# Graph attention layer with a feed-forward step: the low halves of four weights on another engine, four banks for the skip tiles, and three smaller edits

## The reference, cut to what matters

```python
xn = layernorm(x)                                   # x: 1250 x 512
q, k, v = [(xn @ W + b).reshape(n, 4, 512) for W, b in ((Wq, bq), (Wk, bk), (Wv, bv))]
alpha = einsum('ehc,ehc->eh', q[dst], k[src]) / sqrt(512)       # 20000 edges
attn = softmax of alpha over the edges with the same dst
agg = segment_sum(attn[:, :, None] * v[src], dst).reshape(n, 2048)
x_attn = agg + xn @ Wskip + bskip
h = x_attn @ Wlin + blin + x_attn[:, :512]
x = x + gamma * (h - mean(h)) / sqrt(var(h) + 1e-5) + beta
z = layernorm(x)
x = x + z, with one-hot results of three small MLPs on decoded bits of z added in columns 80 to 111
```

## Time and profile before

| | |
|---|---|
| median of 3 runs | 1007.43 us (1007.0 to 1008.04) |
| the profiled execution's own time | 1006.13 us |
| its span, first to last instruction | 1004.1 us |
| granted TensorE clock, mean | 0.995 of full speed |
| busy: TensorE, DVE, ACT, POOL | 985.0, 579.6, 337.0, 105.3 us |
| TensorE's share of the chain that ended last | 94% |

### The profile page before, as it was taken

The page is one execution under the profiler, slowest core; times in us unless marked ns, Lnnn a source line. Parts: engine busy times, 40 slices in busy tenths (PEclk is TensorE's granted clock), DMA queues, the critical chain, the costliest instruction groups (busy, mean ns, idle before and its releaser), DMA issues.

```text
span 1004.1 us, 13119 instructions
## 1 busy us (share of the span) xinstructions
PE 985.0 (98%) x4841; PEld 804.6 (80%) x4841; DVE 579.6 (58%) x1224; ACT 337.0 (34%) x530; POOL 105.3 (10%) x232
## 2 busy tenths in 40 slices
PE   9999999999999999999999999999999999999994
PEld 6677767588888888888888888888888888888883
DVE  6999987452455455226454542354455325788786
ACT  4447555102223223114222321133232213445353
POOL 2121101000000000000000000000000000344465
PEclk9999999999999999999999999999999999999997
DMA  9856654400152335004323430161334103443421
GB/s 328 301 193 210 246 187 165 169 1 1 52 189 62 97 98 169 28 1 147 121 79 105 154 88 1 27 214 54 105 79 163 52 1 82 154 125 100 143 82 40
DMA packets 43048, 115.82 MB, mean 115 GB/s; under 512 B 4960, under 2 KB 25306, under 8 KB 39660
## 3 DMA queue, kind: packets, MB, share of 16 engines
q1 hardware_dynamic: 38380, 98.20, 31.3%
q0 software_dynamic: 4608, 16.78, 4.3%
HBM read 70.07 MB, written 44.90 MB: 114 GB/s over the span
## 4 chain that ended last, share of the span: by engine, by line
PE 94%; DVE 3%; DMA 1%; issue 1%; ACT 0%; SPq 0%; DVEq 0%
PE ps_o L1513 10%; PE ps_o L1514 10%; PE ps_o L1515 10%; PE ps_r L1513 9%; PE ps_r L1514 9%; PE ps_r L1515 9%; PE ps_s L1514 9%; PE ps_s L1515 9%; PE ps_s L1513 9%; PE ps_t L1513 2%; PE ps_t L1515 2%; PE ps_t L1514 2%; PE ps_s L1632 1%; PE ps_s L1592 1%; DMA early<-in_Wv 1%
## 5 line engine op out<-in xcount | busy, mean ns | idle before, releaser
L1514 PE MATMUL ps_s<-xT_lo,tT 128*128 128x512 f32 (+1 forms) x480 | 168.7, 351 | 0.0
L1515 PE MATMUL ps_s<-xT_hi,tT 128*128 128x512 f32 (+1 forms) x480 | 168.4, 351 | 0.0
L1513 PE MATMUL ps_s<-xT_hi,tT 128*128 128x512 f32 (+1 forms) x480 | 168.1, 350 | 0.0
L1513 PE MATMUL ps_o<-y,pT 128*128 128x512 f32 x380 | 148.6, 391 | 0.0
L1514 PE MATMUL ps_o<-y,pT 128*128 128x512 f32 x380 | 148.0, 389 | 0.0
L1515 PE MATMUL ps_o<-y,pT 128*128 128x512 f32 x380 | 148.0, 389 | 0.0
L881 ACT ACTIVATE prob<-prob,nbias 128x1250 f32<-128x1250 f32 x40 | 53.7, 1342 | 267.8 <-DVE nbias L1277 267.8
L1271 DVE CUSTOM_DVE_ANT_0 prob<-ps_s,maskb 128x1250 f32<-128x1250 f32 x40 | 58.2, 1455 | 128.0 <-issue 127.8
L1513 PEld LDWEIGHTS ps_s<-xT_hi,tT 128*128 128x128 f32 x480 | 90.6, 189 | 14.3 <-issue 0.3
L1514 PEld LDWEIGHTS ps_s<-xT_lo,tT 128*128 128x128 f32 x480 | 90.6, 189 | 13.9
L1515 PEld LDWEIGHTS ps_s<-xT_hi,tT 128*128 128x128 f32 x480 | 90.7, 189 | 12.6
(11 more groups left out here) (289 smaller groups left out, 1761.1 us busy)
## 6 DMA issues: line engine op xcount, KB each, us to landing
regrouped<-prob SPq DMA_DIRECT2D x156, 160.0 KB, 2.8
whole<-regrouped SPq DMA_DIRECT2D x39, 640.0 KB, 3.9
products<-prod_parts POOLq DMA_DIRECT2D x32, 512.0 KB, 3.8
gbuf<-products SPq DMA_DIRECT2D x4, 2048.0 KB, 8.2
mbuf<-products SPq DMA_DIRECT2D x4, 2048.0 KB, 9.1
stage<-in_Wskip SPq DMA_DIRECT2D x4, 1024.0 KB, 5.3
stage<-in_Wq SPq DMA_DIRECT2D x3, 1024.0 KB, 5.2
stage<-in_Wk SPq DMA_DIRECT2D x3, 1024.0 KB, 5.9
```

Source lines behind the costliest of these rows:

```text
L1513: nc.tensor.matmul(out_, a[0], b[0], start=start, stop=False)
L1514: nc.tensor.matmul(out_, a[0], b[1], start=False, stop=False)
L1515: return nc.tensor.matmul(out_, a[1], b[0], start=False, stop=stop)
```

## The change

- **Low halves.** For `n` = 4, 9, 14, 19, POOL forms the low half, by one operation of 128x2048 behind its store of block 0 of products 1, 4, 7 and 10. DVE no longer does.
- **Skip banks.** The skip tiles go through four banks (ps_r 0, ps_o, ps_t 0, ps_t 1). TensorE waits for DVE's adds from tile 4 on, and once for the last saved block of the products.
- **Counts of product 1.** Part 0 after block 1, part 1 after block 2, parts 2 and 3 after block 3.
- **Operand 3 in halves.** Its high and low halves are each formed by columns in two operations, as for operand 2.
- **Tail.** The sum of squares takes the raw row sum (scaled by 512) in place of the mean, so it comes before the mean in ACT's list; the centring on DVE and the second layernorm's factors wait for the mean.
- **Last stores.** Tiles 8 and 9 are stored in three pieces each: the two beside columns 80 to 111 when the row is scaled, and these 32 columns when the results are in, tile 9 first.

```diff
+SKIP_BANKS = 4
@@ skip_bank
-            return ps_r[0:R, 0, :] if t % 2 == 0 else ps_o[0:R, :]
+            return (ps_r[0:R, 0, :], ps_o[0:R, :], ps_t[0:R, 0, :], ps_t[0:R, 1, :])[t % SKIP_BANKS]
@@ sync
+            def store_rest(t):
+                rows = min(R, N - R * t)
+                sp.wait_ge(o_scaled, t + 1)
+                for a, b in ((LO_HI_OUT + 32, D), (0, LO_HI_OUT)):
+                    sp.dma_start(out[R * t:R * t + rows, a:b], acc[0:rows, t, a:b]).then_inc(out_done, 16)
+
+            def store_result(t):
+                rows = min(R, N - R * t)
+                some = slice(LO_HI_OUT, LO_HI_OUT + 32)
                 if t == BY_POOL:
                     sp.wait_ge(o_pool, 1)
                 else:
-                    sp.wait_ge(o_ready, t + 1 if t < BY_POOL else t)
+                    sp.wait_ge(o_ready, t)
+                sp.dma_start(out[R * t:R * t + rows, some], acc[0:rows, t, some]).then_inc(out_done, 16)
...
-            for t in range(NT - 4, NT):
+            for t in range(NT - 4, NT - 2):
                 store(t)
+            for t in range(NT - 2, NT):
+                store_rest(t)
+            for t in (NT - 1, NT - 2):
+                store_result(t)
@@ gpsimd
+            def skip_weight_lo(n):
+
+                pool.wait_ge(hi_ready[n % 2], n // 2)
+                nc.gpsimd.tensor_tensor(opnd[n % 4][1][:], raw(n)[:], opnd[n % 4][0][:].bitcast(F32),
+                                        ALU.subtract).then_inc(split_ready[n % 2], 1)
+
             for p in range(3 * H):
                 for i in range(KC):
                     if p % 3 != K_PROD:
                         store_product(p, i)
+                    if p % 3 == M_PROD and i == 0:
+                        skip_weight_lo(operands(p + 1)[0])
...
-                link(nc.gpsimd.tensor_scalar(veps[0:R, t:t + 1], stats[0:R, t, square:square + 1], 1.0 / D, EPS,
+                link(nc.gpsimd.tensor_scalar(veps[0:R, t:t + 1], stats[0:R, t, square:square + 1], 1.0 / D ** 3, EPS,
@@ scalar
+            def split_hi_halves(n):
+
+                for half, high in enumerate((half_hi[n - 2], hi_ready[n % 2])):
+                    some = half_cols(half)
+                    nc.scalar.activation(opnd[n][0][:, :, some], raw(n)[:, :, some], ACT.Copy).then_inc(high, 1)
+
+            act.wait_ge(diag_ready, 1)
+            split_hi_halves(3)
             act.wait_ge(early_in[0], 16)
-            nc.scalar.activation(opnd[2][0][:, :, half_cols(0)], raw(2)[:, :, half_cols(0)],
...
+            split_hi_halves(2)
@@ h_squares (z_squares in the same way, with res_ready)
                 act.wait_ge(acc_ready, NT * H + t + 1)
+                nc.scalar.activation(junk[0][0:R, :], acc[0:R, t, :], ACT.Square, scale=-float(D), bias=stats[0:R, t, 0:1],
+                                     accum_out=stats[0:R, t, 1:2]).then_inc(h_square, 1)
                 nc.scalar.activation(mv[0:R, t, 0:1], stats[0:R, t, 0:1], ACT.Copy, scale=1.0 / D).then_inc(h_mean, 1)
-                act.wait_ge(h_mean, t + 1)
-                nc.scalar.activation(junk[0:R, :], acc[0:R, t, :], ACT.Square, scale=-1.0, bias=mv[0:R, t, 0:1],
-                                     accum_out=stats[0:R, t, 1:2]).then_inc(h_square, 1)
@@ vector
-            split_lo(1, 1)
+            split_lo_halves(3)
...
-                elif i < 2 and p + 1 < 3 * H:
+                elif i < 2 and p + 1 < 3 * H and p % 3 != M_PROD:
                     split_lo(p + 1, 1 - i)
@@ tensor
                 if 0 < p <= NT and (p, i) != (1, 0):
-                    for some in ((0, 1) if (p, i) == (1, 1) else (i,)):
+                    for some in {(1, 1): (0,), (1, 2): (1,), (1, 3): (2, 3)}.get((p, i), (i,)):
                         count_part(p - 1, some)
...
             skip_part(1, (2, 3))
+            pe.wait_ge(prod_free, 12 * H)
             pe.wait_ge(total_ready, 1)
...
             for t in range(2, NT):
-                pe.wait_ge(skip_free, t - 1)
+                if t >= SKIP_BANKS:
+                    pe.wait_ge(skip_free, t - SKIP_BANKS + 1)
                 skip_part(t, range(KC))
```

More of the change, by code:

```diff
@@ L274, in graph_layer @@
         z_low = [put(f"z_low{i}", [P, Z_LOW], F32) for i in range(2)]
-        junk = put("junk", [P, D], BF16)
+        junk = [put(f"junk{i}", [P, D], BF16) for i in range(2)]
         flag_pool = put("flag_pool", [P, 4], F32)
@@ L347, in graph_layer @@
         split_ready = [sem(f"split_ready{i}") for i in range(2)]
-        half_hi, half_split = sem("half_hi"), sem("half_split")
+        half_hi, half_split = [sem(f"half_hi{n}") for n in (2, 3)], sem("half_split")
         prod_done, prod_hi, prod_free = sem("prod_done"), sem("prod_hi"), sem("prod_free")
@@ L552, in load_x @@
                              x[R * t:R * t + rows, :]).then_inc(xres_in[2 if t == NT - 1 else t % 2], 16)
-            def store(t):
+            def store_rest(t):
                 rows = min(R, N - R * t)
+                sp.wait_ge(o_scaled, t + 1)
[4 more added lines that the diff above has]
+                some = slice(LO_HI_OUT, LO_HI_OUT + 32)
                 if t == BY_POOL:
@@ L558, in store @@
                 else:
-                    sp.wait_ge(o_ready, t + 1 if t < BY_POOL else t)
+                    sp.wait_ge(o_ready, t)
+                sp.dma_start(out[R * t:R * t + rows, some], acc[0:rows, t, some]).then_inc(out_done, 16)
+            def store(t):
+                rows = min(R, N - R * t)
+                sp.wait_ge(o_ready, t + 1)
                 sp.dma_start(out[R * t:R * t + rows, :], acc[0:rows, t, :]).then_inc(out_done, 16)
@@ L576, in _ @@
                     load_x(NT - 1)
-            for t in range(NT - 4, NT):
+            for t in range(NT - 4, NT - 2):
                 store(t)
-            sp.wait_ge(out_done, 16 * NT)
+            for t in range(NT - 2, NT):
+                store_rest(t)
+            for t in (NT - 1, NT - 2):
+                store_result(t)
+            sp.wait_ge(out_done, 16 * (NT + 4))
         @block.gpsimd
@@ L658, in z_factors @@
                 nc.gpsimd.tensor_scalar(stats[0:R, t, 4:5], rstd[0:R, t:t + 1], 1.0, None, ALU.add)
+                pool.wait_ge(z_mean, t + 1)
                 nc.gpsimd.tensor_scalar(nmr[0:R, t:t + 1], mv[0:R, t, 1:2], rstd[0:R, t:t + 1], -1.0,
@@ L750, in split_hi @@
                     if n % 2 == odd:
[L751 to L758, removed]
+                        act.wait_ge(stage_in[odd], 16 * (n // 2 - 1))
+                        act.wait_ge(prod_done, 4 * last_use(n - 4) + 4)
                         nc.scalar.activation(opnd[n % 4][0][:], raw(n)[:], ACT.Copy).then_inc(hi_ready[odd], 1)
@@ L891, in h_squares @@
                 act.wait_ge(acc_ready, NT * H + t + 1)
+                nc.scalar.activation(junk[0][0:R, :], acc[0:R, t, :], ACT.Square, scale=-float(D), bias=stats[0:R, t, 0:1],
+                                     accum_out=stats[0:R, t, 1:2]).then_inc(h_square, 1)
                 nc.scalar.activation(mv[0:R, t, 0:1], stats[0:R, t, 0:1], ACT.Copy, scale=1.0 / D).then_inc(h_mean, 1)
-                act.wait_ge(h_mean, t + 1)
-                nc.scalar.activation(junk[0:R, :], acc[0:R, t, :], ACT.Square, scale=-1.0, bias=mv[0:R, t, 0:1],
-                                     accum_out=stats[0:R, t, 1:2]).then_inc(h_square, 1)
             def z_squares(t):
                 act.wait_ge(res_ready, t + 1)
+                nc.scalar.activation(junk[1][0:R, :], acc[0:R, t, :], ACT.Square, scale=-float(D), bias=stats[0:R, t, 2:3],
+                                     accum_out=stats[0:R, t, 3:4]).then_inc(z_square, 1)
                 nc.scalar.activation(mv[0:R, t, 1:2], stats[0:R, t, 2:3], ACT.Copy, scale=1.0 / D).then_inc(z_mean, 1)
-                act.wait_ge(z_mean, t + 1)
-                nc.scalar.activation(junk[0:R, :], acc[0:R, t, :], ACT.Square, scale=-1.0, bias=mv[0:R, t, 1:2],
-                                     accum_out=stats[0:R, t, 3:4]).then_inc(z_square, 1)
             def scale_rows(t):
@@ L999, in split_lo, with split_lo_halves @@
                                                 ALU.subtract).then_inc(split_ready[odd], 1)
-            def split_halves():
-                for some, high, low in ((half_cols(0), half_hi, half_split), (half_cols(1), hi_ready[0], split_ready[0])):
+            def split_lo_halves(n):
+                for half, high in enumerate((half_hi[n - 2], hi_ready[n % 2])):
+                    some = half_cols(half)
                     dve.wait_ge(high, 1)
-                    nc.vector.tensor_tensor(opnd[2][1][:, :, some], raw(2)[:, :, some],
-                                            opnd[2][0][:, :, some].bitcast(F32), ALU.subtract).then_inc(low, 1)
+                    ins = nc.vector.tensor_tensor(opnd[n][1][:, :, some], raw(n)[:, :, some],
+                                                  opnd[n][0][:, :, some].bitcast(F32), ALU.subtract)
+                    if half:
+                        ins.then_inc(split_ready[n % 2], 1)
```

(7 more changed lines are left out.)

4 lines of the change are left out of this document (removed).

## The result

The changed kernel takes 1012.99 us (median of 6 runs, 1012.5 to 1013.16), the kernel before 1008.18 beside it (6 runs, 1007.0 to 1008.7): ratio 1.0049, 95% interval 1.0036 to 1.0061. It is slower by more than the 0.2% that the prediction set, and outside its range (1004.2 to 1010.6). The profiled execution took 1012.94 us for a span of 1010.8; the one of before had a span of 1004.1, so the two traces are 6.7 us apart.

What follows compares the result with a forecast made beforehand. TensorE was taken as the bound, busy 985.0 of 1004.1 us, with gains only where it waits. Terms 0.95 + 1.25 + 0.2 - 2.5 + 0.5 - 0.85 = -0.45 us gave 1007.0 from 1007.43; range 1004.2 to 1010.6.

Steps and rivals of the forecast that it cites:

- Whom POOL's pass stops: POOL and DVE: whoever comes first keeps the other out if DVE reads two SBUF operands, as `onehot_src` does.
- the 0.95 predicted: Low half on POOL in product 1: `onehot_src` waits for the pass, so product 2 starts 0.95 us later.
- Products 7 and 10 at nothing: POOL's passes there cost nothing; in product 7 the one-hots end 0.5 us before TensorE wants them.
- TensorE waits there instead, about 4 us in one piece: Product 1's moved counts: the 1.22 us wait goes, TensorE waits before product 2 instead, at no net cost.
- POOL's duration: One POOL operation of 128x2048 takes 4.45 us, bounds 4.2 to 5.2, from the slope of shorter additions.
- The second rival: POOL's pass is much longer and becomes the bound: 1011.1 us with a pass of 6.0; chance 0.21.
- Product 4: Low half on POOL there: `onehot_src` stands until the pass ends, making the kernel 1.25 us later.
- The transfer behind it: Behind product 4, weight 11 loads later and delays ACT's high half: 0.2 us later, bounds nothing to 0.5.
- Skip banks: In the skip, four banks remove TensorE's whole wait for DVE's first add: 2.5 us earlier, other bound 0.
- Counts: Moved counts of product 1 gain nothing, since product 2 cannot start before the last one-hots.
- Tail: Layernorms of tile 9: centring waits 0.72 us longer for the mean, second layernorm gains 0.24; 0.5 us later.
- Last stores: At the kernel's end, smaller last stores shorten SP's wait: 0.85 us earlier, nearest bounds nothing and 2.0.

Runs made afterwards that it cites:

- the form that does not wait: Changed kernel with the five one-hot operations of product 1's batch 2 also writing an accumulator nobody reads; 1010.87 us, ratio 1.0033.
- the four pieces: Changed kernel with POOL's pass of 2048 columns cut into four operations of 512; 1014.45 us, ratio 1.0077.
- the pair of versions: Changed kernel with low halves back on DVE, first layernorm's mean behind the squares (1005.18 us, ratio 0.9977) or ahead of them (1004.16 us, ratio 0.9972).

## Why the prediction was wrong

- **Whom POOL's pass stops.** This is the step that failed: "whoever comes first keeps the other out, if the DVE operation reads two SBUF operands". The condition was too narrow. `onehot_dst` has one, and was kept out for 4.4 to 5.0 us in products 1, 7 and 10 (5.99 less 1.20, 5.37 less 0.98, 5.48 less 0.5). The prediction named `onehot_dst` only the other way round, as what might keep POOL out, at 0.7 us and inside a rival. Held in batch 2, DVE could not save block 1, nor begin batch 3, so these came after the pass: product 2 2.56 late (3.04 less 0.48) for the 0.95 predicted. With the form that does not wait, the sequence was the predicted one: the save done, `onehot_src` kept out until POOL ends, product 2 1.03 late against DVE's list, for 0.95 predicted.
- **Products 7 and 10 at nothing.** The same step. The cover of 0.5 us was worked out for a pass that DVE meets with its `onehot_src`; it met it one batch earlier, with `onehot_dst`, and the digits, the save and the last batch moved behind it. In product 7 ACT then stood 4.06 us for the digits (to 129.61), and its own list ran late: the high half of the next weight starts at 135.39 for 125.87, 9.5 later where TensorE is 7.7 later. DVE, which stood 1.38 us for a save of ACT at 133.08, ran as late with it, and its one-hots are what TensorE waits for before product 9. The lag rose by 0.7 at the turn behind product 7 and by 0.9 at product 9, and by 0.9 more through product 10: 2.6 us in all that stood in the sum as 0.
- **What TensorE does after a long wait.** No term of the sum had it. Around 3.6 us of waits (2.27 and 1.36) the granted clock fell, and the first block of product 2 ran at the lower clock, 1.72 us (4.76 less 3.04). "TensorE waits there instead, about 4 us in one piece" was written with no price for the piece.
- **POOL's duration**, 4.45 predicted, is 4.67; the Trainium skill's 4497 ns (GPSIMD Engine Reference, section 3.1) is nearer to the estimate than to the row, whose output is fp32r. The second rival's cause, a pass of over 5.2, did not occur; its sign did, and nearly its size (1011.1), for another reason.
- **Product 4**, 1.25 predicted, is 1.42 (6.18 less 4.76): factors quick again, L638 in 0.24 us for 1.99, `onehot_src` kept out until POOL's end. **The transfer behind it**, 0.2 predicted, is 0.8 (6.98 less 6.18): the weight was asked for at 84.41 and ACT, which stood 3.22 us for it, began at 90.85, so it took some 6.4 us, over the upper bound of 5.9.
- **Skip banks**, 2.5 predicted, is 2.74, and 2.75 alone. **Counts** and **operand 3** at nothing: the counts measured so alone, the operand's halves were not tried by themselves.
- **Tail**, 0.5 later: 0.44 by the pair of versions. From the last output matmul to SP's last issue it is 13.35, for 12.86 before. **Last stores**, 0.85 earlier: 0.38 in the changed kernel (3.19 before, 2.81 after, from the issue to the end). The wait did shrink as predicted (1.1, "near 1.2"), but another, of 0.8 us and for TensorE's queue, stands behind it where it was 0.2.
- **The sum** was -0.45 and the traces say +6.7: product 1 +1.6, its clock +1.7, product 4 and the transfer +0.8, products 7 to 10 +2.6, stores +0.45, the start +0.48, less 0.24 in the skip and 0.2 in the attention. The medians are only 4.8 apart, since the profiled execution of before was one of the quicker ones, as the prediction said. The start is counted as one term, but it is not passed on one for one: the version with the low halves back on DVE was 2.2 late at the first counts and 0.65 early at product 2.
- **Two small slips in its sums.** By its own bounds the forecast spans from 1005.2, not 1005.4, and 1009.4 is reached from a pass of some 5.4 us, not 5.6. Neither bears on the rest.

## What to carry to other kernels

Before moving an operation to POOL, look at the list of DVE under it. What stood here was more than the operations with two SBUF inputs: the one-input `onehot_dst`, whose rows show some 0.25 ns a column, stood too, and once the digits. Let such a slope be the warning, though no run tried where it ends. Then walk DVE's list from the moment when POOL starts, not from the moment when DVE becomes free, and count everything queued behind the first operation that stops, on the engines that read its results too. DVE gained 9 us of passes here and lost 16 in stretched one-hots, so its busy time went up.

A wait of TensorE can have a second price, the block behind it at the lower clock, 1.4 to 1.7 us here. Where a change makes a wait longer, put that price in the range.

## What the runs showed of the hardware that was not expected

- A 16-bit one-input DVE operation of 0.30 us stood 4.70 to 5.26 us, until POOL's pass of 4.7 had ended, though its row begins up to 0.46 us before that of the pass. The same operation with an accumulator takes 0.33 from one to the next and did not stand at all. That this is a remedy is not shown, since the version that had it did not give the kernel's results.
- Four POOL operations in a row kept one DVE operation out to the end of the fourth in products 1, 4 and 10. In product 7 the two engines took turns, one DVE operation behind each, and DVE's next save still came behind the fourth.
- The clock's fall behind a wait of 1.2 to 1.7 us came in some profiles and not in others: at 1.21 us with the banks alone and not at 1.22 in the kernel before, at 1.71 in product 4 with product 1's low half on DVE and not at 1.73 in the changed kernel. It came in the one profile with a wait of 2.16 us (the accumulator) and in all four with 3.1 to 3.7 us in one or two parts (the changed kernel, POOL's passes alone, the old counts, the four pieces). What decides it at the shorter waits is left open.
